# Self attention on one core: weighted sums and totals gathered in two places of a group

## The reference, cut to what matters

```python
qk = x @ w_attn.T + b_attn
q, k = jnp.split(qk, 2, axis=-1)
q, k, v = (_heads(q), _heads(k), _heads(x))
scores = jnp.einsum('bhqd,bhkd->bhqk', q, k) * scale
scores = jnp.where(causal, scores, -jnp.inf)
y_ar = jnp.einsum('bhqk,bhkd->bhqd', jax.nn.softmax(scores, axis=-1), v)
# a second, linear attention follows on v - y_ar ("memory"), then w_proj for both
```

## Time and profile before

| | us |
|---|---|
| median of 3 runs (lowest, highest) | 1807.82 (1803.44, 1814.86) |
| the profiled execution | 1807.97 |
| its span, from the first to the last instruction | 1806.2 |

### The profile page before, as it was taken

One profiled execution on the slowest core, in us unless ns is written; L12 is line 12 of the kernel. 1 busy time (PEld: TensorE's weight loads), 2 busy tenths in 40 slices (PEclk: granted clock), 3 DMA queues, 4 the chain that ended last, 5 costly groups with the idle time before them and its releaser, 6 DMA issues.

```text
span 1806.2 us, 30853 instructions
## 1 busy us (share of the span) xinstructions
PE 1710.4 (95%) x10602; PEld 1112.9 (62%) x10602; DVE 1266.0 (70%) x2792; ACT 980.7 (54%) x1931; POOL 1181.3 (65%) x969
## 2 busy tenths in 40 slices
PE   5999999999999889999988899999999999999997
PEld 4666666666666547877853456565565656556566
DVE  5677677676777657777856776767767676776744
ACT  3555555555555532433345566565656655566554
POOL 2556556565564554754467887887788687778873
PEclk9999999999999869999988999999999999999999
DMA  7455565565554464576625544435434443543200
GB/s 203 137 157 161 141 160 158 143 165 145 152 154 125 122 206 131 197 204 184 189 73 145 148 107 109 117 86 138 106 99 114 117 109 86 146 107 83 72 35 24
DMA packets 167272, 237.29 MB, mean 131 GB/s; under 512 B 22086, under 2 KB 73286, under 8 KB 167116
## 3 DMA queue, kind: packets, MB, share of 16 engines
q1 hardware_dynamic: 167116, 235.31, 47.1%
HBM read 91.57 MB, written 41.94 MB: 74 GB/s over the span
## 4 chain that ended last, share of the span: by engine, by line
PE 65%; POOL 14%; DVE 7%; issue 5%; ACT 4%; DMA 3%; SPq 1%; POOLq 0%; ACTq 0%; DVEq 0%
POOL cross_added L1920 9%; PE bank L201 8%; PE bank L1606 7%; PE bank L202 6%; PE bank L203 6%; PE bank L296 5%; PE bank L351 5%; PE bank L338 4%; PE bank L1447 4%; PE bank L1418 4%; PE bank L1479 3%; DVE cross_negmax L1428 2%; PE bank L316 2%; DVE bank L1761 2%; PE bank L899 1%
## 5 line engine op out<-in xcount | busy, mean ns | idle before, releaser
L1428 DVE TENSOR_REDUCE cross_negmax<-bank 128x1 f32<-128x512 f32 x512 | 339.7, 676 | 156.2 <-PE bank L1418 151.6
L530 DVE CUSTOM_DVE_ANT_0 bank<-bank,future 128x128 f32<-128x128 f32 (+3 forms) x512 | 246.8, 489 | 172.3 <-PE bank L338 171.6
L1690 ACT ACTIVATE cpt<-bank 128x512 f32<-128x512 f32 x512 | 296.5, 595 | 129.9 <-PE bank L1447 126.4
L412 ACT ACTIVATE pt<-bank 128x256 f32<-128x256 f32 (+3 forms) x512 | 224.5, 441 | 256.8 <-PE bank L296 256.2
L1920 POOL TENSOR_TENSOR cross_added<-cross_added,cpt 128x2048 f32<-128x2048 f32 x64 | 293.5, 4587 | 14.5 <-ACT cpt L1690 14.1
L1447 PE MATMUL bank<-cqk 98*128 98x512 f32 x512 | 228.7, 447 | 24.7 <-ACT cpt L1690 23.8
L594 POOL TENSOR_SCALAR_AFFINE_SELECT pt<-pt 128x512 f32<-128x512 f32 x128 | 81.4, 636 | 252.5 <-ACT pt L412 252.5
L1418 PE MATMUL bank<-cqk 96*128 96x512 f32 x512 | 211.4, 416 | 15.9 <-DVE cross_negmax L1428 13.2
L1920 POOL TENSOR_TENSOR cross_added<-cpt,cpt 128x2048 f32<-128x2048 f32 x32 | 146.8, 4588 | 96.5 <-ACT cpt L1690 96.4
L201 PE MATMUL bank<-xt_hi,w_hi 128*128 128x512 f32 x384 | 168.7, 439 | 16.5 <-DVE w_lo L488 13.6
L296 PE MATMUL bank<-qk 98*128 98x256 f32 (+2 forms) x512 | 181.3, 358 | 2.0 <-ACT pt L412 1.6
(11 more groups left out here) (203 smaller groups left out, 3665.1 us busy)
## 6 DMA issues: line engine op xcount, KB each, us to landing
qk<-stage SPq DMA_DIRECT2D x384, 128.0 KB, 2.3
cqk<-cstage SPq DMA_DIRECT2D x384, 128.0 KB, 2.4
scratch_memory<-memory SPq DMA_DIRECT2D x32, 512.0 KB, 3.8
ma<-scratch_memory SPq DMA_DIRECT2D x32, 512.0 KB, 4.0
raw<-in_x_t SPq DMA_DIRECT2D x32, 256.0 KB, 2.8
v<-in_x SPq DMA_DIRECT2D x32, 256.0 KB, 3.2
scratch_y_ar<-y_ar SPq DMA_DIRECT2D x32, 256.0 KB, 2.2
my_ar<-scratch_y_ar SPq DMA_DIRECT2D x32, 256.0 KB, 4.4
```

What stands on the lines that cost most here:

```text
L412: act.activation(s.pt[step % 3][:, j, 0:SEQ - first], sh.bank[2 + n % 2][:, first - q0:SEQ - q0], ACT.Exp, scale=SCALE_SELF).then_inc(s.ac ...
L530: dve.tensor_tensor_reduce(out=scores, in0=scores, in1=sh.future[:, SEQ - P * (qt + 1):SEQ], scale=-1.0, scalar=-NEG, op0=ALU.add, op1=ALU ...
L1428: dve.reduce_max(s.negmax[gm % 2][:, col:col + 1], max_bank(sh, m)[:, :], AX, negate=True).then_inc(s.dve_max, 1)
L1690: act.activation(s.pt[step % 3][:, j, :], sh.bank[2 + n % 2][:, :], ACT.Exp, scale=SCALE_CROSS).then_inc(s.act_exp, 1)
```

## The change

The weighted sums keep their number and their order, and move:

- steps 0 and 1 of a group (512 and 384 columns) stand together in (2,3) of the same group, a slot without a projection. Before they stood in (2,1) and (3,1);
- steps 2 and 3 (256 and 128 columns) stand together in (0,3) of the next group, behind that slot's projection, and directly behind them the totals. Before, these three stood in (0,1), (1,1) and (1,0).

ACT's copy `y_raw` moves from (1,3) to (1,0), and DVE's four reciprocals and the product each move one slot earlier.

```diff
-        if j == 1 and 0 <= n // PER - 2 < NG * TILES:
-            self_weighted(pe, s, sh, n // PER - 2)
+
+        if (kt, j) == (2, 3) and 0 <= g < NG:
+            self_weighted(pe, s, sh, TILES * g)
+            self_weighted(pe, s, sh, TILES * g + 1)
         if (kt, j) in PROJECTED:
             on, i = PROJECTED[kt, j]
             if 0 <= g + on < NG:
                 self_project(pe, s, sh, g + on, i)
-        if kt == 1 and j == 0 and 0 <= g - 1 < NG:
+        if kt == 0 and j == 3 and 0 <= g - 1 < NG:
             d = g - 1
+            self_weighted(pe, s, sh, TILES * g - 2)
+            self_weighted(pe, s, sh, TILES * g - 1)
             pe.wait_ge(s.pool_add, 3 * (d + 1))
             pe.wait_ge(s.act_copied, d + 1)
             pe.wait_ge(s.dve_k, min(d + 4, NG))
@@ self_scalar
-        if kt == 1 and j == (3 if g < NG else 2) and 0 <= g - 1 < NG:
+        if kt == 1 and j == 0 and 0 <= g - 1 < NG:
             act.wait_ge(s.pe_pv, TILES * g)
@@ self_vector
-        k = PER * kt + j - PER - 1
+        k = PER * kt + j - PER
         if 0 <= k < TILES and 0 <= g - 1 < NG:
             sums = sh.bank[6][:, tile_of(k)]
             dve.wait_ge(s.pe_tot, g)
```

## The result

| | us |
|---|---|
| before, median of 20 runs | 1809.4 |
| after, median of 20 runs | 1802.39 |
| ratio | 0.9962, 95% interval 0.9948 to 0.9976 |
| profiled execution after, its span | 1798.7 |

The change makes the kernel 0.38% faster, 1809.4 x 0.0038 = 6.9 us (4.3 to 9.4). The forecast was 1804, 4 us less; its range of 1796 to 1816 holds the result.

A forecast was written before the change was run, and what follows sets the result against it. PE, busy 497.66 of 500 us, sets the pace, but DVE's chain equally bounds the stretch before the transpose. -5.0 us over 28 groups and +1 in the last three, against 1807.97, gave 1804 us; range 1796 to 1816, about 80%.

The forecast's parts named there:

- PE and DVE are both at the limit at the transpose: Self attention, transpose of the negated maxima: both engines arrive together, so work taken from PE alone can't shorten the 7.14 us before.
- An island's fixed part is 0.335 us, joined ones don't pay it inside: Runs of matmuls with 32 output rows: entry, start-up and exit cost 0.335 us; joining saves 1.0 us PE work per group.
- Rival 2: Joined sums writing the same bank still pay start-up, about 0.14 us each: +0.42 us a group, 1816 us; 12%.
- E to T by DVE's chain, 6.57: First record after the totals' matmuls (E) to transpose of negated maxima (T): DVE's maxima, reciprocals, product take 6.57 us, before 7.14.
- T to E, 12.3: From the transpose to the first record after the next totals, PE's work sets the time: 12.3 us, 11.91 before.
- Period 18.87: One group of 16 slots in self attention takes 18.87 us against 19.05.
- Rival 3: DVE's chain before the transpose stays at 7.14 us: period 19.44, kernel 1820 us; 14%.
- PE waits 0.88 us a group: Before the transpose PE stands still 0.88 us, since DVE's chain takes 6.57 us and PE's work 5.69.
- Waits for the shift rows go: After the transpose 0.85 us more PE work covers their transfer, so PE's 2.5 us of waits (0.09 a group) go.
- The clock holds: Granted clock stays 1.00 to 600 us despite PE's new stall; the rival, a clock drop to 1948 us, had 3%.
- The last groups cost +1 us: Three last groups, without projections: 512 + 128 columns move into PE's stretch, partly at half clock; 0 to +2, taken as +1.
- 28 groups: Self attention: the 0.18 us saved per period was counted over 28 groups, 5.0 us less.

The follow-up runs named there:

- split run: The changed kernel with the projection piece of (0,3) set between the sums of steps 2 and 3 and the totals, three islands a group: 1812.46 us, ratio 1.0030.
- two pairs of profiles: The kernel before and the changed kernel, each run unchanged once more for a second profile: 1804.72 us before, 1805.91 after.

## Why the prediction was right

- *PE and DVE are both at the limit at the transpose*: right. In the changed kernel halving the reciprocals removes the wait and gives 22 us; moving the sums out without the totals costs 17.
- *An island's fixed part is 0.335 us, joined ones don't pay it inside*: right. The split run shows 0.33 by period. Rival 2, which lets joined sums of one bank pay the start-up, is out: 1.64 us for 1.49 us of columns is one start-up of 0.15, not two.
- *E to T by DVE's chain, 6.57*: measured 6.54. The saving in it is two terms, DVE's wait for late scores and one maximum of 256 columns that has become one of 128; the prediction's "one ahead and one behind" counts the latter twice, its sum doesn't. *T to E, 12.3*: measured 12.35. *Period 18.87*: measured 18.90. Rival 3 would have needed over 6.75.
- *PE waits 0.88 us a group*: it was ready 0.68 us ahead of T (323.40 to 324.08), with the rest of the slack spent in waits of 0.2 for DVE's maximum ahead of the scores of (2,2).
- *Waits for the shift rows go*: right, 2.5 us became 0.4.
- *The clock holds*: right, 1.00 to 560 us with 3.4% idle, and so in the run with only the sums moved, with 6.3% (468.68 of 500 us busy). The Trainium skill, TensorE: Matmul & The Clock Gate, A second HAM failure mode, tells of a clock that swings because PE idles briefly but often; that does not show in these rows.
- *The last groups cost +1 us*: wrong. The term took the stretch at half clock as it was and had the moved columns run in it; the two pairs of profiles show a gain of 1.8 us, with a mean granted clock of 0.75 and 0.79 in place of 0.64. That the clock makes the gain is likely, no run isolates it.
- *28 groups*: the first group, counted at nothing, gained 0.9 us.

The last two terms, 2.8 and 0.9 us, less the 1.0 by which 28 periods gained less than the 5.0 of the sum (4.0 in the mean of the pairs), are the step from 4 us to some 6.8 in the profiles. The mechanism carries about 4 us of the gain in the steady groups and 0.9 in the first; the rest is not shown to come from it, and that the forecast came within 2 us of the measured 1802 is in part luck.

## What to carry to other kernels

Runs of matmuls with 32 output rows that stand next to each other pay their switch once (0.33 us here), but joining them moves work, and the stretch that it leaves can be held by another engine. Cut the period at the waits between engines, write both engines' sum for each stretch, and look where the freed time comes to lie: here it lay in front of one wait, and a piece of independent work moved from behind the wait to ahead of it took in 15 more microseconds, while the same move cost 6 where there was no wait to fill and where it left three slots so close together that PE waited for ACT. Before calling a time between two events the need of a transfer, check that the engine was idle in it. And before calling a wait a cost, look whether the matmuls keep their rhythm: a weight load's wait of 0.6 us in every group cost nothing here, one of 0.2 us cost 0.28.

## What the hardware showed that I had not expected

A busy average of 72% on DVE went with a stretch of 5.8 us in every 19 without any idle time, and that stretch set the end. The granted clock in the first group without projections went back to 2.4 GHz after 3.4 us at half clock in the changed kernel (two profiles) and after 10.2 in the one before (two profiles), with PE busy for 90 to 96% of the first ten microseconds in both; in the next group it took the changed kernel 13.6 us in one profile and 6.8 in the other.
